# Two-layer graph kernel: another order of the ramp's matmuls and loads, and the small vectors on GpSimd's DMA queue

## The reference

```python
Xw = X @ Wv + bv
e = leaky_relu((Xw @ aw[:d])[:, None, :] + (Xw @ aw[d:])[:, :, None] + ab, 0.2)
alpha = A * exp(e)
transition = alpha / (sum(alpha, -1) + 1e-12)
H = 0; Xk = X
for k in range(3):
    H = H + Xk @ Wk[k] + bk[k]
    Xk = transition @ Xk
x = layernorm(x + relu(H))
x = layernorm(x + (adj @ x) @ w)
```

## Time and profile before

| | us |
|---|---|
| median of 3 runs | 275.37 |
| lowest, highest | 274.53, 275.59 |
| the profiled execution's own time | 274.77 |
| its span, first to last instruction | 273.0 |
| PE busy in the span | 266.3 (98%) |
| DVE, ACT, POOL busy | 218.0, 187.8, 194.8 |

### The profile page before, as it was taken

How to read it: one execution, slowest core, us unless ns; L and a number is a source line. 1 busy time by engine, 2 the same in 40 slices (tenths; PEclk the granted TensorE clock), 3 DMA queues, 4 the chain that set the end, 5 groups by cost and what they waited for, 6 DMA issues and landing times.

```text
span 273.0 us, 6038 instructions
## 1 busy us (share of the span) xinstructions
PE 266.3 (98%) x1899; PEld 247.3 (91%) x1899; DVE 218.0 (80%) x613; ACT 187.8 (69%) x427; POOL 194.8 (71%) x419
## 2 busy tenths in 40 slices
PE   7999999999999999999999999999999999999992
PEld 4899999999999999999999999999999999999991
DVE  0877698888889888888988888898888889688984
ACT  2788667777666777766677776667777666666652
POOL 2566548777877777787777878777788877557664
PEclk9999999999999999999999999999999999999999
DMA  7958347647488389454973488654994449722304
GB/s 209 275 174 95 73 115 123 141 117 149 151 144 117 100 135 148 155 154 143 135 97 104 150 154 148 137 156 89 90 168 90 117 115 115 115 66 77 118 2 154
DMA packets 28614, 34.91 MB, mean 128 GB/s; under 512 B 7075, under 2 KB 16422, under 8 KB 28582
## 3 DMA queue, kind: packets, MB, share of 16 engines
q1 hardware_dynamic: 27872, 33.99, 59.3%
q10 hardware_dynamic: 710, 0.53, 0.6%
HBM read 26.09 MB, written 8.42 MB: 126 GB/s over the span
## 4 chain that ended last, share of the span: by engine, by line
PE 94%; DVE 2%; DMA 2%; POOL 0%; issue 0%; ACT 0%; DVEq 0%
PE ps_v L1053 30%; PE ps_y L1053 16%; PE ps_out L1053 14%; PE ps_h L1053 11%; PE ps_agg L1224 10%; PE ps_v L1161 3%; PE ps_v L1165 3%; PE ps_v L1163 3%; DMA WY_sb<-Wk_dram 2%; PE ps_agg L1053 1%; PE ps_y L1079 1%; PE ps_v L1079 1%; DVE WX_lo L870 0%; DVE ps_v L634 0%; PE ps_y L1208 0%; POOL late_rstd L989 0%
## 5 line engine op out<-in xcount | busy, mean ns | idle before, releaser
L963 POOL TENSOR_TENSOR alpha<-exps,adjs 128x256 f32<-128x256 f32 x31 | 22.9, 738 | 35.4 <-ACT exps L449 35.4
L1053 PE MATMUL ps_v<-WX_hi,XT_hi 128*128 128x512 f32 (+1 forms) x128 | 47.7, 372 | 0.0
L1053 PE MATMUL ps_v<-WX_lo,XT_hi 128*128 128x512 f32 (+1 forms) x128 | 47.4, 371 | 0.0
L1053 PE MATMUL ps_v<-WX_hi,XT_lo 128*128 128x512 f32 (+1 forms) x128 | 47.3, 370 | 0.0
L951 POOL TENSOR_TENSOR XT_lo<-xt,XT_hi 128x512 fp32r<-128x512 f32 x32 | 41.5, 1297 | 3.0 <-ACT XT_hi L406 1.6
L481 ACT ACTIVATE y<-res,offset,rstd 128x256 f32<-128x256 f32 x62 | 33.6, 591 | 0.9 <-POOL offset L922 0.9
L967 POOL TENSOR_TENSOR alpha_lo<-alpha,alpha_hi 128x256 fp32r<-128x256 f32 x31 | 22.8, 736 | 15.9 <-ACT alpha_hi L458 15.9
L1053 PE MATMUL ps_y<-WY_hi,XT_hi 128*128 128x258 f32 x112 | 34.1, 304 | 0.0
L1224 PEld LDWEIGHTS ps_agg<-adjs,y 128*128 128x128 f32 x248 | 32.0, 191 | 2.2
L1224 PE MATMUL ps_agg<-adjs,y 128*128 128x128 f32 x248 | 32.6, 274 | 0.0
L1053 PE MATMUL ps_out<-w_hi,agg_hi 128*128 128x256 f32 x112 | 31.6, 282 | 0.0
(11 more groups left out here) (168 smaller groups left out, 843.9 us busy)
## 6 DMA issues: line engine op xcount, KB each, us to landing
xt<-xt_dram SPq DMA_DIRECT2D x32, 256.0 KB, 5.9
nodes<-nodes_dram SPq DMA_DIRECT2D x32, 256.0 KB, 6.1
out_dram<-out_sb SPq DMA_DIRECT2D x30, 256.0 KB, 5.9
adjs<-adjs_dram SPq DMA_DIRECT2D x32, 128.0 KB, 6.0
spread<-si_rows_dram SPq DMA_DIRECT2D x29, 128.0 KB, 5.3
W_sb<-Wk_dram SPq DMA_DIRECT2D x2, 256.0 KB, 3.9
si_rows_dram<-scores SPq DMA_DIRECT2D x29, 1.0 KB, 4.1
WY_sb<-Wk_dram ACTq DMA_DIRECT2D x1, 256.0 KB, 4.1
```

The lines of the kernel that those rows point to most:

```text
L963: pool.tensor_tensor(alpha[:], exps[:], adjs_sb[k % 5][:], ALU.mult).then_inc(alpha_ready, 1)
L1053: last = pe.matmul(to, a, b, start=start and n == 0, stop=stop and n == 2, skip_group_check=True)
```

## The change

On TensorE the ramp is put in another order, with one warm-up matmul fewer. On SP, WvT is no longer issued, and `load_xt(4)` also waits for `y_done`, since hop 2 of pair 0 now reads xt(0) last. ScalarE issues WvT first, then Wk(2), then bk. GpSimd issues vectors and ab at the head of its list. The lists of ScalarE and VectorE follow the new order.

```diff
@@ sync
                 if k == 4:
+                    sp.wait_ge(y_done, 1)
                     sp.wait_ge(v1_done, 1)
...
             load_xt(0)
-            sp.dma_start(WvT_sb[:], WvT.rearrange("(c p) n -> p c n", p=P)).then_inc(WvT_loaded, DMA)
             load_Wk(1)
             sp.wait_ge(xt_loaded[0], DMA)
             load_Wk(0)
@@ scalar
+            act.dma_start(WvT_sb[:], WvT.rearrange("(c p) n -> p c n", p=P)).then_inc(WvT_loaded, DMA)
             act.dma_start(WY_sb[:, :, 0:D], Wk[2].rearrange("(c p) n -> p c n", p=P)).then_inc(Wk_loaded[2], DMA)
-            act.dma_start(vectors_sb[:].rearrange("p c n -> p (c n)"), vectors).then_inc(vectors_loaded, DMA)
             act.dma_start(bk_sb[:], bk).then_inc(bk_loaded, DMA)
-            act.dma_start(ab_col[:], ab.partition_broadcast(P)).then_inc(ab_loaded, DMA)
...
             xt_hi(0)
+            first_scores()
             wx_hi(0)
-            v2_hi(0)
             xt_hi(1)
-            first_scores()
-            xt_hi(2)
             leaky_of(0)
             exponentials(0)
+            v2_hi(0)
+            alpha_hi_of(0)
+            xt_hi(2)
             xt_hi(3)
-            alpha_hi_of(0)
             wx_hi(1)
             scores_of(1)
@@ vector: the copies of u, the split of WY and WX_lo of hop 0 stood ahead of the rest; now
+            dve.wait_ge(u_done, 1)
+            dve.tensor_copy(W1_sb[:, :, D:D + 2], ps_u).then_inc(u_ready, 1)
+            dve.tensor_copy(WY_sb[:, :, D:D + 2], ps_u).then_inc(u_ready, 1)
+            bias_of_hops()
             shift_of_scores()
+            (wait for Wk[2]; WY_hi, WY_lo)
+            first_hop1()
+            (wait for WX_hi_ready[0]; WX_lo of hop 0)
+            first_alpha()
             v2_lo(0)
-            bias_of_hops()
-            first_hop1()
-            first_alpha()
+            first_alpha_lo()
             first_hop0()
-            first_alpha_lo()
             v2_lo(1)
@@ gpsimd, ahead of its memsets
+            pool.dma_start(vectors_sb[:].rearrange("p c n -> p (c n)"), vectors).then_inc(vectors_loaded, DMA)
+            pool.dma_start(ab_col[:], ab.partition_broadcast(P)).then_inc(ab_loaded, DMA)
@@ tensor
-            keep_warm(ps_v[:, 0], 9)
+            keep_warm(ps_v[:, 0], 8)
+            score_weights()
+            sum_of_biases()
+            score_shift()
+            first_hop1(0)
+            first_hop1(1)
             first_hop2(0)
-            score_weights()
-            first_hop2(1)
-            first_hop1(0)
-            score_shift()
-            first_hop1(1)
-            sum_of_biases()
             pe.wait_ge(identity_ready, 1)
             spread_scores(0)
+            first_hop2(1)
             hop0(0)
             hop2_and_scores(1)
```

More of the change, by code:

```diff
@@ L592, in _ @@
             dve.memset(ones[:], 1.0).then_inc(ones_ready, 1)
[L594 to L603, removed]
             def shift_of_scores():
@@ L857, in split_w @@
                 dve.tensor_tensor(w_lo[:], w_sb[:], w_hi[:].bitcast(F32), ALU.subtract).then_inc(w_ready, 1)
+            dve.wait_ge(u_done, 1)
+            dve.tensor_copy(W1_sb[:, :, D:D + 2], ps_u).then_inc(u_ready, 1)
+            dve.tensor_copy(WY_sb[:, :, D:D + 2], ps_u).then_inc(u_ready, 1)
+            bias_of_hops()
             shift_of_scores()
+            dve.wait_ge(u_ready, 2)
+            dve.wait_ge(Wk_loaded[2], DMA)
+            dve.tensor_copy(WY_hi[:], WY_sb[:]).then_inc(WY_hi_ready, 1)
+            dve.wait_ge(WY_hi_ready, 1)
+            dve.tensor_tensor(WY_lo[:], WY_sb[:], WY_hi[:].bitcast(F32), ALU.subtract).then_inc(WY_ready, 1)
+            first_hop1()
+            dve.wait_ge(WX_hi_ready[0], 1)
+            dve.tensor_tensor(WX_lo[:, :, 1], W0_sb[:], WX_hi[:, :, 1].bitcast(F32), ALU.subtract).then_inc(WX_ready[0], 1)
+            first_alpha()
             v2_lo(0)
-            bias_of_hops()
-            first_hop1()
-            first_alpha()
+            first_alpha_lo()
             first_hop0()
-            first_alpha_lo()
             v2_lo(1)
```

## The result

The changed kernel takes 279.16 us (median of 4 runs, 278.97 to 279.18), the kernel before 275.06 us (4 runs, 274.53 to 275.59): ratio 1.0149, 95% interval 1.0133 to 1.0164, 4.1 us slower. The forecast was 276.1 us, in a range up to 277.8. No run in this document had to be left out as one in a slow state, but the runs of an experiment can fall into groups, and the lists show them.

A forecast was written before the change was run, and what follows sets the result against it. TensorE's ramp was taken as the bound, everything after pair 1's hop 2 following its end. With bk at 6.5 us hop 1 starts at 7.29 us, that end comes 0.73 us later: 275.37 + 0.73 = 276.1 us, range 274.8 to 277.8.

The forecast's parts named there:

- the one on the clock: TensorE's warm-up: its last matmuls already run at 2.4 GHz, so eight seem enough; costed at nothing.
- rival C: Pause and small matmuls let TensorE fall to 1.2 GHz: +1.96 us for hop 1's two products, 278.1 us; chance 0.1.
- vectors, a term that was mis-sized: Load on GpSimd's queue, issued at about 0.7 us, taken to land at 5 us, within 2.9 to 6.3 us.
- Rival B: Vectors land late on GpSimd's queue: at 6.3 us T grows by 1.6 us, giving 276.9 us; chance 0.2.
- bk, a bound that did not bind: Load third on ScalarE's queue, landing at 6.5 us; `sum_of_biases`, ahead of hop 1, cannot start before it.
- S: Start of `first_hop1(0)` on TensorE, forecast at 7.29 us; break-even at 6.56 us.
- The order itself: TensorE's reordered ramp puts work not needed at once ahead, behind a late load: T 0.73 us later.
- T: End of pair 1's hop 2 on TensorE, S + 7.16: forecast 14.45 us against 13.72 before.
- the stretch behind T: From T to `propagate_v1(0)`, via ScalarE and VectorE, 4.3 us: same operations and order, moving only as T moves.
- The cover on ScalarE of 0.2 us: ScalarE's earlier work ends at V + 5.0, before pair 1's scores at V + 5.23; each further 0.1 us costs 0.1.
- V: End of hop 1 on TensorE, S + 1.96, forecast at 9.25 us.
- The rest of the covers: Other moved work costed at nothing: adjs(0) covered by 0.7 us, plus SP's later issues, GpSimd's setup, VectorE's WY halves.

The follow-up runs named there:

- experiment 4: Kernel before with vectors and ab issued by GpSimd at the head of its list: 275.32 us, ratio 1.0009.
- experiment 3: Kernel before with eight warm-up matmuls instead of nine: ratio 1.0031; seven of ten runs 274.65 to 275.14 us, the others 276.51, 278.54 and 278.63.
- 11: Kernel before with five warm-up matmuls and nothing else changed: 278.25, 279.00, 278.47, 277.84 us, ratio 1.0128.
- experiment 5: Changed kernel with vectors issued first on ScalarE's queue, ahead of WvT: 278.73, 278.85, 278.82, 280.55 us, ratio 1.0164.
- experiment 6: Changed kernel with twelve warm-up matmuls instead of eight: median 277.37 us, ratio 1.0076.
- experiment 12: The version of experiment 8 with 12 instead of 9 warm-up matmuls: twelve runs from 275.34 to 276.36 us, ratio 1.0032.
- experiment 9: Kernel before in its instruction orders, with the changed kernel's loads and 12 warm-up matmuls: seven runs from 275.64 to 276.10 us, ratio 1.0031.
- 7: Kernel before in its instruction orders, with the changed kernel's loads and nine warm-up matmuls: median 276.56 us, ratio 1.0074.
- experiment 1: Changed kernel with the ninth warm-up matmul put back: 279.24, 279.23, 279.29 and 277.67 us, ratio 1.0142.
- experiment 10: Version of experiment 6 with two more warm-up matmuls behind score_weights and one behind score_shift: 276.54 to 279.74 us, ratio 1.0117.
- experiment 2: Changed kernel with sixteen warm-up matmuls instead of eight: median 276.81 us, ratio 1.007.
- 8: Changed kernel with vectors first on ScalarE's queue, 9 warm-up matmuls, hop 1 right behind score_weights, biases behind the first products: ratio 1.0077.

## Why the prediction was wrong

**The step that failed is the one on the clock.** It said "So eight seem enough here" and gave rival C a chance of 0.1. It had named the danger itself (from 4.1 to 6.55 us only matmuls of two columns) and then argued it away with the pause from 4.32 to 4.99 us in the kernel before. What failed is the inference from one execution, in which the clock had risen after 3.7 us, inside the warm-up. In others it had not risen when eight or nine matmuls were done (fastest 583 ns in the changed kernel, 584 ns in experiment 4), and with eight of them the pause that follows is longer. With one warm-up matmul fewer, that same ramp loses the clock in 3 of 10 runs (experiment 3), with five in 4 of 4 (11). The kernel before stood close to an edge which its trace did not show, on the good side of it: none of its 70 runs beside the experiments took over 275.63 us. Measured: 3.37 us in place of nothing, and 1.96 us in rival C's own price, since at 1.2 GHz `score_weights`, biases and shift take longer too: (1.86 + 1.14 + 0.52 + 3.66) - (1.05 + 0.62 + 0.31 + 1.87) = 3.3 us. Rival C's mechanism was right in the main: it spoke of a fall, and in three of the four runs the clock was not raised in time at all. Its time of 278.1 us was 1.1 us short, and the range ended below it.

**vectors, a term that was mis-sized.** Taken to land at 5 us, they land at 5.90, within the bounds of 2.9 to 6.3: the issue begins at 1.25, not 0.7 us, takes 0.76 us, and landing takes 4.65 us from its start. Rival B named them. They count twice: `score_weights` starts 0.8 us later than forecast, and the pause in which the clock is lost is longer by as much. The page DMA: Bandwidth & Descriptors of the Trainium skill (Anatomy of one DMA — SWDGE (gpsimd) path) gives a fixed cost of about 2 us for a DMA on GpSimd's path; measured here, with the DMA engines full beside it, it is 4.65 us, and the measurement decides.

**bk, a bound that did not bind.** The step had the four loads end at 6.4 us, bk at 6.5, and bk set S. The loads end at 6.1 us at the latest. bk came at 6.57 us in experiment 5, close to what was said, but with vectors at 5.9 us it is there before `score_weights` has ended: in experiment 6 the biases follow with no wait. Vectors set S, by the prediction's own formula at 5.90 + 0.1 + 0.98 + 0.74 = 7.72 us; it was 7.89, mostly since `score_shift` takes 0.31 us in its new place and not 0.12.

**The order itself: its size right, in part by luck.** The forecast was "T = 14.45 us, 0.73 us later"; with the clock granted (experiment 6) `propagate_v1(0)` comes 0.81 us later. But the terms are off and make up for each other. S is 7.89 and not 7.29 us, and the end of hop 1 9.76 and not 9.25. T, the end of the last matmul of pair 1's hop 2, is 14.42 + 0.28 = 14.70 us, 0.98 us later than before; it would be later still if small groups did not overlap where the sum had put them end to end (4.94 us from hop 1 to T instead of 5.20). And the stretch behind T, which the prediction took as unchanged, is shorter: from pair 1's scores to `propagate_v1(0)` 18.84 - 14.87 = 3.97 us against 18.03 - 13.74 = 4.29 before.

**The cover on ScalarE of 0.2 us did not hold.** It reads pair 1's scores 14.87 - 9.76 = 5.11 us after hop 1, at the end of a row of its own work, where V + 5.0 was said and T came at V + 4.94: 0.14 us later than T + 0.03. The chain goes there through VectorE's product with alpha, 0.79 us against 0.43 us for the same instruction in the kernel before. Two rows of experiment 6 show what was beside it, first GpSimd, then VectorE:

```profile
11.16 1.42 POOL L952 TENSOR_TENSOR XT_lo<-xt,XT_hi 128x512 fp32r<-128x512 f32 x1 [3.27 <-ACT XT_hi L405]
...
12.08 0.78 DVE L604 TENSOR_TENSOR alpha<-exps,adjs 128x256 f32<-128x256 f32 x1 [0.65 <-ACT exps L448]
```

GpSimd's subtraction ends at 12.58 us, 0.28 us before VectorE's product ends; in the changed kernel it ends at 14.53 + 1.42 = 15.95 and the product at 16.24. In the kernel before it had ended (at 12.04 us) when the product began, and in experiment 12 (at 11.83 us) too; there the product takes 0.43 and 0.42 us. The page SBUF — State Buffer of the Trainium skill (SBUF: two separate sides) says that a VectorE operation with two SBUF inputs and a GpSimd operation that reads SBUF exclude each other for a whole instruction; the four traces agree: where the two meet, the product ends 0.28 or 0.29 us after GpSimd's instruction has ended. It costs the path the 0.14 us above, and the forecast had only looked at each engine's own order. The same meeting shortens the stretch behind T. VectorE's subtraction WX_lo, on the chain there, takes 1.06 us before, beside 0.51 us of GpSimd's product for the next pair, and 0.85 us in experiment 6, beside 0.30 us of it.

**The rest of the covers held**: SP's later issues, the later adjs(0), GpSimd's setup behind its two issues and VectorE's halves of WY appear in no wait of TensorE.

What stays open: in the new order with twelve warm-up matmuls 5 of 7 runs fell (6), in the old order with the same loads and as many none of 7 (9), though TensorE can pause for some tenths of a us in both. (Twelve end at 5.3 us when the clock rises near 4.4, and real work waits until 5.9 in the one and 5.8 in the other.) The old order goes on with full-width products, the new one with two-column ones; that these make the short pause longer for the clock is argued from that pair, and 12 shows that without a pause they do no harm. It was not tried by itself. Nor was the length of the warm-up parted from that of the pause in experiments 3 and 11. And the cause of the remaining 1.5 us in the changed kernel with twelve is argued, not shown: no run with fourteen, say, tested it.

## What to carry to other kernels

An edge of the ramp is seen in many runs, not in one trace: before moving TensorE's first work or taking a warm-up matmul away, count the time from the end of the warm-up to the first dense matmuls, and bridge it to the latest landing. Twelve matmuls that nobody reads cost 0.2 us here at most (experiment 9 starts at 6.05 us, 7 at 5.83), and the pause without them up to 3.6 us. A fixed count is a compromise: twelve end at 5.3 us where the clock rises early and at 6.05 where it rises late, and sixteen ran 1.2 us too long. And before putting a small group of matmuls first because more depends on it, check that its own data are the first to land: the old order's advantage was a product that could start on what came first.

## What the runs showed of the hardware

- The moment at which the clock rises differs from run to run with the same instructions ahead of it: it came between 3.7 and 4.3 us in the traces of the kernel before and of experiment 1, near 4.4 us in experiment 10 and near 6.5 in experiment 2, all of them busy with the same warm-up matmuls from 0.8 us on. The Trainium skill, page TensorE: Matmul & The Clock Gate (What's actually happening), says that the low level is the default and that activity releases it, at a point that varies between runs; the traces agree.
- Runs fall into groups by how long the clock stays low. Where it fell for about 3.4 us they are 1.5 to 1.9 us above the best (profiled runs of experiments 7, 8 and 10, low from 7.9 to 11.3, 7.4 to 10.8 and 7.9 to 11.2 us). They are 3 to 4 us above it where it fell for about 6.8 us (experiments 1 and 5, low from 7.4 to 14.2 and 7.1 to 13.9 us), and where it was not raised before the pause and stays low until 12 or 13 us (the changed kernel, experiments 3 and 11). The last kind leaves no mark in the column of the granted clock.
- A DMA of 128 rows of 24 bytes takes 4.6 us from issue to landing behind a 256 KB load on ScalarE's queue (kernel before), 4.3 to 4.8 us alone on GpSimd's (changed kernel, experiments 1, 2, 4, 6, 7, 9, 10), and 3.0 us as the first of ScalarE's queue (5, 8, 12). Put ahead of WvT it has that load land at 5.29 instead of 4.2 us, of which 0.44 us is the issue.
